# Cross-attention by autocorrelation with a mixture-of-experts layer: skewed copies folded by VectorE, one product a sum instead of two

## The reference, cut to what matters

```python
qf = jnp.fft.rfft(qt)
kf = jnp.fft.rfft(kt)
c = qf.real * kf.real + 1j * -(qf.imag * kf.imag)
corr = jnp.fft.irfft(c, n=Lq)
...
mean_value = jnp.mean(corr, axis=(1, 2))
weights, delay = jax.lax.top_k(mean_value, top_k)
tmp_corr = jax.nn.softmax(weights, axis=-1)
```

## Time and profile before

| what | value |
|---|---|
| three runs | 997.3, 999.38, 1002.05 us; median 999.38 |
| profiled execution, its own time | 996.96 us |
| its span in the trace | 995.1 us |
| granted PE clock, share of full | 0.999 |
| PE busy | 983.5 us (99%) |
| DVE, ACT, POOL busy | 655.4, 380.2, 473.6 us |
| moved by DMA | 216.93 MB, mean 218 GB/s |

### The profile page before, as it was taken

The page is one execution under the profiler, slowest core; times in us unless marked ns, Lnnn a source line. Parts: engine busy times, 40 slices in busy tenths (PEclk is TensorE's granted clock), DMA queues, the critical chain, the costliest instruction groups (busy, mean ns, idle before and its releaser), DMA issues.

```text
span 995.1 us, 21034 instructions
## 1 busy us (share of the span) xinstructions
PE 983.5 (99%) x6750; PEld 601.8 (60%) x6750; DVE 655.4 (66%) x1506; ACT 380.2 (38%) x776; POOL 473.6 (48%) x540
## 2 busy tenths in 40 slices
PE   9999999999999999989999999999999999999998
PEld 7776644444444445557777778777777544444443
DVE  4977788874498898965555555555555476676766
ACT  3646454343545333324444444444444311111111
POOL 0725412131145477654445444444543376666672
PEclk9999999999999999999999999999999999999999
DMA  9735867868562711558889988889988578999675
GB/s 348 259 126 196 295 193 233 233 192 237 175 180 96 222 64 64 127 147 248 251 248 239 256 242 249 242 249 233 261 250 230 169 238 260 313 260 307 187 226 177
DMA packets 175483, 216.93 MB, mean 218 GB/s; under 512 B 101096, under 2 KB 112232, under 8 KB 174376
## 3 DMA queue, kind: packets, MB, share of 16 engines
q1 hardware_dynamic: 151640, 136.95, 46.8%
q0 software_dynamic: 23760, 78.79, 26.8%
HBM read 123.67 MB, written 69.22 MB: 194 GB/s over the span
## 4 chain that ended last, share of the span: by engine, by line
PE 81%; DVE 9%; DMA 4%; issue 3%; ACT 2%; SPq 0%; POOL 0%; DVEq 0%; ACTq 0%; POOLq 0%
PE bank L1068 19%; PE bank L941 13%; PE bank L1131 13%; PE bank L1092 9%; PE bank L957 7%; PE bank L1144 6%; PE bank L1051 5%; PE bank L716 2%; PE bank L1082 2%; PE bank L793 1%; DMA arena<-in_x 1%; DMA arena<-xr_dram 1%; PE bank L696 1%; DVE arena L1855 1%; DVE arena L1622 1%
## 5 line engine op out<-in xcount | busy, mean ns | idle before, releaser
L1068 PE MATMUL bank<-arena 128*128 x1716 | 211.0, 273 | 0.9 <-issue 0.7
L941 PE MATMUL bank<-arena 128*128 128x512 f16 x888 | 202.3, 379 | 0.5 <-DVE arena L1616 0.2
L1068 PEld LDWEIGHTS bank<-arena 128*128 128x128 f16 x1716 | 163.0, 98 | 26.1 <-issue 1.4
L2139 POOL DMA_INDIRECT arena<-y_dram,arena x128 | 135.7, 1060 | 77.9 <-issue 28.9
L2082 POOL DMA_INDIRECT arena<-xr_dram,arena x143 | 139.6, 976 | 59.4 <-issue 48.2
L941 PEld LDWEIGHTS bank<-arena 128*128 128x128 f16 x888 | 87.2, 99 | 100.9 <-DVE arena L1616 0.7
L1131 PE MATMUL bank<-arena 128*128 128x512 f16 x648 | 144.1, 379 | 0.6 <-DMA arena<-xr_dram 0.6
L1092 PE MATMUL bank<-arena 128*128 x429 | 115.4, 378 | 0.5 <-ACT arena L1401 0.5
L1884 DVE SCALAR_TENSOR_TENSOR arena<-bank,arena 128x128 f32<-128x128 f32 x143 | 41.7, 292 | 109.5 <-ACT arena L1390 108.7
L1338 ACT ACTIVATE arena<-arena 128x512 f16<-128x512 f32 x64 | 40.3, 629 | 184.4 <-DVE arena L1616 104.5
L1951 DVE SCALAR_TENSOR_TENSOR arena<-arena 128x512 f32<-128x512 f32 x128 | 95.3, 749 | 23.1 <-DMA arena<-y_dram,arena 20.5
(11 more groups left out here) (227 smaller groups left out, 1318.9 us busy)
## 6 DMA issues: line engine op xcount, KB each, us to landing
y_dram<-arena SPq DMA_DIRECT2D x143, 256.0 KB
arena<-in_x SPq DMA_DIRECT2D x8, 1024.0 KB, 12.0
xr_dram<-arena SPq DMA_DIRECT2D x16, 512.0 KB, 3.9
x_dram<-arena SPq DMA_DIRECT2D x8, 1024.0 KB, 5.6
arena<-in_gu_w SPq DMA_DIRECT2D x16, 512.0 KB, 3.5
out<-arena SPq DMA_DIRECT2D x32, 256.0 KB, 3.8
arena<-x_dram SPq DMA_DIRECT2D x5, 1024.0 KB, 6.0
arena<-in_gu_w POOLq DMA_DIRECT2D x8, 512.0 KB, 4.7
```

What stands on the lines that cost most here:

```text
L941: last = mm(bank[half][:, :], (gu_hi_s, gu_lo_s)[wp][:, c, at:at + H], xt[:, xv * KC + kc, :], start=(n == 0), stop=(n == 3 * KC - 1))
L1068: last = mm(gate_up_bank(s, s)[:, 0:2 * H], rows[:, xv * KC + kc, :], only((gu_hi_r, gu_lo_r)[wp], e, slice(kc * 2 * H, (kc + 1) * 2 * H)) ...
L2139: pool.indirect_dma_start(out=ybuf[n % RING][:, e, :], out_offset=None, in_=y_dram[:, :], in_offset=bass.IndirectOffsetOnAxis(ap=row_of[:, ...
```

## The change

It does the following.

- The two skewed copies are read by halves: partitions 0 to 63 of both tensors (now `skew_near`, `skew_far`) hold the copy shifted one way, its first and its second 64 rows; partitions 64 to 127 hold the other copy in the same manner. For batch 0, where the two lie side by side, one DMA of 64 partitions fills both (`skew_both`); for batch 1 each DMA is split in two: four early reads by GpSimd for two, six late ones by SP for three.
- VectorE adds `skew_far` onto `skew_near` (`fold_part`, a tensor_tensor in f32): for batch 0 in three steps of 768, 512 and 128 + 640 columns, for batch 1 in two, of 1,280 and of 128 + 640.
- `skewed_sum` is one product, with a column of ones and one of ones and minus ones.
- PE's order changes: batch 0's sums are gathered behind the folds, the transposes of block 4 come ahead of the first sums, value parts move behind; the mean correlation comes one value part earlier. In batch 1 the first three sums stand at the end of chunk 0, nine in the first half of chunk 1 and four in its second.
- VectorE's router constants move from ahead of block 5's normalisation to behind `vo_low(0)`.
- GpSimd: blocks 0 to 3 first, then (once the even parts are saved) three tiles of block 4, the first weights, the last tile of block 4 and block 5, then the early reads of batch 1, and only then block 6.

```diff
-SUM_AT = {(0, 0, 10): 1, (0, 0, 11): 2, **{(0, 1, n): i + 3 for i, n in enumerate((0, 1, 3, 4, 6, 7, 9, 10))},
-          (1, 0, 11): 0, **{(1, 1, n): n + 11 for n in range(NA - 11)}}
+SUM_AT = {**{(0, 1, n): n - 8 for n in range(9, 12)}, **{(1, 0, n): n + 4 for n in range(7)},
+          (1, 0, 10): 0, (1, 0, 11): 11, **{(1, 1, n): n + 12 for n in range(NA - 12)}}
+FOLD = P // 2
...
-                sp.dma_start(skew_c[0][:, max(lo - M, 0):hi - M], skewed(0, 2 * M - 1, PTW - 1, max(lo - M, 0), hi - M)
-                             ).then_inc(s_sk[0], 16)
-                sp.dma_start(skew_d[0][:, max(lo, M):hi], skewed(0, 1, PTW + 1, max(lo, M), hi)).then_inc(s_sk[0], 16)
+                sp.dma_start(skew_both[0:FOLD, :, max(lo - M, 0):hi - M],
+                             skewed(0, 2 * M - 1, PTW - 1, max(lo - M, 0), hi - M)).then_inc(s_sk[0], 16)
+                sp.dma_start(skew_both[FOLD:P, :, max(lo, M):hi], skewed(0, 1, PTW + 1, max(lo, M), hi)).then_inc(s_sk[0], 16)
...
-                mm(dst, skew_c[b][:, a * P:a * P + P], c_sb[:, C_ONES + 2 - SUM_W:C_ONES + 2], start=True, stop=False)
-                return mm(dst, skew_d[b][:, a * P:a * P + P], c_sb[:, C_ONES + 4 - SUM_W:C_ONES + 4], start=False, stop=True)
+                return mm(dst, skew_near[b][:, a * P:a * P + P], c_sb[:, C_ONES + 4 - SUM_W:C_ONES + 4],
+                          start=True, stop=True)
...
             second_g(0)
-            pe.wait_ge(s_sk[0], 32)
-            second_g_and_sum(1, (1, 2))
-            skewed_sum(0, 3)
+            second_g(1)
             turn_first(4)
-            for a in (4, 5, 6):
+            pe.wait_ge(s_fold, 1)
+            second_g_and_sum(2, (1, 2, 3, 4))
+            for a in (5, 6):
                 skewed_sum(0, a)
-            pe.wait_ge(s_sk[0], 64)
-            second_g_and_sum(2, (7, 8))
-            second_g_and_sum(3, (9, 10))
+            pe.wait_ge(s_fold, 2)
+            second_g_and_sum(3, (7, 8, 9, 10))
...
-            pe.wait_ge(s_sk2[0], 48)
-            value_part_and_sum(0, (0, 11, 12))
-            summed = value_part_and_sum(1, (13, 14, 15))
+            value_part(0, bank[5], 0)
+            pe.wait_ge(s_fold, 3)
+            for a in (0, *range(11, NA)):
+                summed = skewed_sum(0, a)
             summed.then_inc(s_u, 1)
-            value_part(0, bank[5], 2)
+            value_part(0, bank[5], 1)
             pe.wait_ge(s_tables, 32)
             pe.wait_ge(s_mm_sb, 14)
             even_parts(0)
+            value_part(0, bank[5], 2)
+            mean_correlation(0)
             value_part(0, bank[5], 3)
-            mean_correlation(0)
...
-                    if g == half == 0 and n == 10:
-                        pe.wait_ge(s_sk[1], 32)
+                    if g == 0 and half == 1 and n == 9:
+                        pe.wait_ge(s_fold, 4)
                         pe.wait_ge(s_pt_sb, 7)
-                    if g == 1 and half == 0 and n == 11:
-                        pe.wait_ge(s_sk2[1], 48)
+                    if g == 1 and half == 0 and n == 10:
+                        pe.wait_ge(s_fold, 5)
...
+            def fold_part(b, lo, hi):
+
+                near = skew_near[b][:, lo:hi]
+                return V.tensor_tensor(near, near, skew_far[b][:, lo:hi], ALU.add)
+
+            def fold_late(b):
+
+                dve.wait_ge(s_sk2[b], 96 if b else 48)
+                fold_part(b, 0, M)
+                fold_part(b, EARLY - M, L).then_inc(s_fold, 1)
...
             normalise(4)
-            dve.wait_ge(s_misc, 64)
...
+            for n, (lo, hi) in enumerate(STEPS[0]):
+                dve.wait_ge(s_sk[0], 32 * (n + 1))
+                fold_part(0, max(lo, M) if n == 0 else lo - M, hi - M).then_inc(s_fold, 1)
             V.memset(ones_row[0:1, :], 1.0)
...
             normalise(5)
+            fold_late(0)
             save_sums(0)
...
                     x1_tile(ATTEND[g], 2, 6)
+                if g == 0:
+                    fold_late(1)
                 dve.wait_ge(s_shh, g + 1)
...
             x1_moments(1)
+            dve.wait_ge(s_sk[1], 64)
+            fold_part(1, M, EARLY - M).then_inc(s_fold, 1)
             shared_weights_lo(1)
...
-            for q in range(5):
+            for q in range(HALF):
                 add_bo(q)
+            pool.wait_ge(s_ev_sb, 3)
+            add_bo(4, (0, 1, 2))
             pool.wait_ge(s_mm, 18)
             pool.wait_ge(s_st[0], 16)
             for n in range(2):
                 shared_weights_in(n)
+            add_bo(4, (3,))
             add_bo(5)
-            pool.wait_ge(s_lo0, TB)
-            add_bo(6)
             pool.wait_ge(s_pte, 16)
             pool.wait_ge(s_u, 1)
             pool.wait_ge(s_mm, 28)
-            pool.dma_start(skew_c[1][:, 0:EARLY - M], skewed(1, 2 * M - 1, PTW - 1, 0, EARLY - M)).then_inc(s_sk[1], 16)
-            pool.dma_start(skew_d[1][:, M:EARLY], skewed(1, 1, PTW + 1, M, EARLY)).then_inc(s_sk[1], 16)
+            for v, dst in enumerate((skew_near[1], skew_far[1])):
+                pool.dma_start(dst[0:FOLD, 0:EARLY - M], skewed_half(1, 2 * M - 1, PTW - 1, 0, EARLY - M, v)
+                               ).then_inc(s_sk[1], 16)
+                pool.dma_start(dst[FOLD:P, M:EARLY], skewed_half(1, 1, PTW + 1, M, EARLY, v)).then_inc(s_sk[1], 16)
+            pool.wait_ge(s_lo0, TB)
+            add_bo(6)
             pool.wait_ge(s_wlo, 1)
             shared_weights_in(2)
             add_bo(7)
...
-            pool.wait_ge(s_sk2[1], 48)
+            pool.wait_ge(s_sk2[1], 96)
```

More of the change, by code:

```diff
@@ L106, in constants @@
     c[:, C_ID:C_ID + P] = eye
-    c[:, C_ONES:C_ONES + 4] = [1, 1, 1, -1]
+    c[:, C_ONES:C_ONES + 4] = 1
+    c[FOLD:, C_ONES + 3] = -1
     c[0, C_J0] = 1
@@ L176, in build @@
         xnT = [view(o + 64 * KB, [KC, BLK]), view(o + 72 * KB, [KC, BLK])]
-        skew_c = [view(o + 80 * KB, [L]), view(o + 88 * KB, [L])]
-        skew_d = [view(o + 88 * KB, [L]), view(24 * KB, [L])]
+        skew_near = [view(o + 80 * KB, [L]), view(o + 88 * KB, [L])]
+        skew_far = [view(o + 88 * KB, [L]), view(24 * KB, [L])]
+        skew_both = view(o + 80 * KB, [2, L])
         xtb_c = view(o + 80 * KB, [2, 2 * KC, BLK], F16)
@@ L320, in skewed, with skewed_half @@
         def skewed(b, start, pitch, first, end):
-            return bass.AP(pt_dram, b * P * PTW + start + first, [[pitch, P], [1, end - first]])
+            return bass.AP(pt_dram, b * P * PTW + start + first, [[pitch, FOLD], [FOLD * pitch, 2], [1, end - first]])
+        def skewed_half(b, start, pitch, first, end, v):
+            return bass.AP(pt_dram, b * P * PTW + start + v * FOLD * pitch + first, [[pitch, FOLD], [1, end - first]])
         s_const, s_tables, s_kw2 = sem("identity_in"), sem("tables_in"), sem("wk_in_2")
@@ L472, in skew_late @@
                 sp.wait_ge(s_ptw[b], 16 * (2 if b else len(STEPS[0]) + 2))
-                sp.dma_start(skew_c[b][:, EARLY - M:L], skewed(b, 2 * M - 1, PTW - 1, EARLY - M, L)).then_inc(s_sk2[b], 16)
-                sp.dma_start(skew_d[b][:, EARLY:L], skewed(b, 1, PTW + 1, EARLY, L)).then_inc(s_sk2[b], 16)
-                sp.dma_start(skew_d[b][:, 0:M], skewed(b, 1, PTW + 1, 0, M)).then_inc(s_sk2[b], 16)
+                if b == 0:
+                    sp.dma_start(skew_both[0:FOLD, :, EARLY - M:L], skewed(0, 2 * M - 1, PTW - 1, EARLY - M, L)
+                                 ).then_inc(s_sk2[0], 16)
+                    sp.dma_start(skew_both[FOLD:P, :, EARLY:L], skewed(0, 1, PTW + 1, EARLY, L)).then_inc(s_sk2[0], 16)
+                    sp.dma_start(skew_both[FOLD:P, :, 0:M], skewed(0, 1, PTW + 1, 0, M)).then_inc(s_sk2[0], 16)
+                else:
+                    for v, dst in enumerate((skew_near[1], skew_far[1])):
+                        sp.dma_start(dst[0:FOLD, EARLY - M:L], skewed_half(1, 2 * M - 1, PTW - 1, EARLY - M, L, v)
+                                     ).then_inc(s_sk2[1], 16)
+                        sp.dma_start(dst[FOLD:P, EARLY:L], skewed_half(1, 1, PTW + 1, EARLY, L, v)).then_inc(s_sk2[1], 16)
+                        sp.dma_start(dst[FOLD:P, 0:M], skewed_half(1, 1, PTW + 1, 0, M, v)).then_inc(s_sk2[1], 16)
             def candidates_in(b):
@@ L744, in second_g_and_sum @@
                                 lambda k: column(kT, k, 1), tiles)
-            def value_part_and_sum(c, tiles):
-                return project_and_sum(bank[5][:, c * M:c * M + M], lambda k: wv_sb[:, k, c * P:c * P + P],
-                                       lambda k: column(ctx_sb, k, 0), tiles)
             def second_k(c):
@@ L1561, in _ @@
             vo_low(0)
+            dve.wait_ge(s_misc, 64)
+            dve.wait_ge(s_const, 16)
+            r3 = rt32.rearrange("p (k e) -> p k e", k=KC)
+            link.done(V.tensor_scalar(rt_hi, r3, WS, None, ALU.mult))
+            V.scalar_tensor_tensor(rt_lo, r3, WS, rt_hi, ALU.mult, ALU.subtract).then_inc(s_rt, 1)
+            V.tensor_copy(id16, c_sb[:, C_ID:C_ID + P]).then_inc(s_rt, 1)
```

(10 more changed lines are left out.)

17 lines of the change are left out of this document (3 added, 14 removed).

## The result

The changed kernel took 1013.83 us (median of 6 runs, 1011.41 to 1019.65), the kernel before beside it 999.18 us (6 runs, 997.30 to 1002.65): ratio 1.0143, 95% interval 1.0118 to 1.0167. Forecast were 999.8 us and a range of 995.5 to 1003.0.

A forecast was written before the change was run, and what follows sets the result against it. TensorE, 99% busy, was taken as the bound, but batch 1's chain over GpSimd, ScalarE and VectorE as deciding: +1.6 us there, -1.24 us behind it, +0.4 on 999.38 gives 999.8 us, range 995.5 to 1003.

The forecast's parts named there:

- Folds, batch 0: VectorE's folds in batch 0: 2.5 us of work, each paying up to one 1 us wait; PE loses 0.2 and 2.2 us.
- Fold 2: Batch 0's second fold on VectorE: ends near 47.1, PE wants it at 47.6, so no wait.
- the late reads: Batch 0's last skewed reads on SP's queue: issued up to 47.16, landing 3.0 us later, at 50.2.
- the late fold: Batch 0's last fold, after block 5's normalisation on VectorE: ends at 52.5, PE ready at 50.3, 2.2 us lost.
- fold 1: Batch 0's first fold, 768 columns on VectorE: ends near 45.3, PE arrives at 45.15, 0.2 us of waiting.
- GpSimd's and VectorE's queue, batch 1: Batch 1's chain from GpSimd's reads, adds and weights 2 through VectorE to block 2's attention product: PE gets there 1.6 us later.
- in time: Batch 1's early reads, last issued at 96.5, land 5.1 us later at 101.6, before VectorE's fold could start at 102.8.
- 1.9 + 1.6 = 3.5: First attention product 1.9 us earlier, that of block 2's second tile 1.6 us later than before: the forecast loss between them.
- Rival 2: Reads of 64 partitions at half rate, batch 1's early ones taking 10.2 us, not 5.1: +2.8 us, 1002.2; chance 0.15.
- Rival 3: PE's order and VectorE's folds in batch 0 lose over 2.2 us, first attention product gains nothing: +2.3 us, 1001.7; chance 0.10.
- the constants moved into VectorE's gap: Router's split and other constants, 9 instructions, in VectorE's idle 4.54 us ahead of 78.39: cost nothing, without that gap 1.5 us.
- rival 1: Neither batch's chain holds PE, so the full saving of 5.9 to 7.1 us comes: 992.3 to 993.5; chance 0.10.

The follow-up runs named there:

- the filled kernel: The changed kernel with idle products on TensorE sized to its waits, two and three in batch 0, 22 short ones in batch 1: 1008.12 us, ratio 1.0081.
- a clean pause of 3.1: The kernel before, with TensorE alone made to wait for VectorE's router constants ahead of a second-batch product, no transfer changed: 1013.79 us, ratio 1.0136.
- the two-queue kernel: The changed kernel with batch 0's transfers to partitions 64 to 127 issued by ScalarE's queue instead of SP's: 1017.50 us, ratio 1.0144.
- The same wait, unfilled and filled: The kernel before with a wait for VectorE's router constants added, alone (1013.79 us) or with three idle products ahead of it (1003.17 us).
- the one with 1.1: The kernel before with the added wait for VectorE's router constants put one second-batch product later, a shorter pause: 1008.15 us, ratio 1.0047.
- the pause kernels: The kernel before with an added TensorE wait: unfilled 1013.79 us, with three idle products ahead 1003.17 us, one product later 1008.15 us.
- the kernel with batch 1 later: The change for batch 1 alone, against the kernel before, fold behind the first low weights and all sums in chunk 1: 1001.92 us, ratio 1.0033.

## Why the prediction was wrong

**Folds, batch 0: "Fold 2 ends near 47.1, PE wants it at 47.6: covered."** This is the step that failed first. I costed the fold and GpSimd's collisions and let the reads land as before. The write ahead of them took 5.0 in place of 2.7 us, its reads were issued at 43.5 in place of 40.9, and fold 2 ended at 49.7. The same goes for "the late reads are issued up to 47.16 and land 3.0 us later, at 50.2": SP issued the last at 50.48, and VectorE began the late fold at 54.57, forecast to end at 52.5. I had expected 2.2 us of waiting there and 0.2 at fold 1; 1.70 at fold 2 and 0.40 there came instead, so the sum of the waiting, 2.1 us, was nearly right and its place wrong.

**The term that the sum lacked: the clock.** The forecast held that a wait costs its length. It can cost more: 5 us of batch 0's 7.4 by the filled kernel, 11 us for a clean pause of 3.1. A pause of 1.70 us set it off in the changed kernel, whose six runs all have a mean clock of 0.985 to 0.990, so the 2.2 us in one piece that I forecast would probably have done so with every landing on time; no run shows that case. The longest pause in the rows of before is 0.70 us, with no fall of the clock behind it: nothing there priced it, but a forecast of 2.2 us of idle time on an engine that had none was the place to ask.

**GpSimd's and VectorE's queue, batch 1.** The chain of queues ran as told, with sizes off, but it held TensorE at another place: the forecast had it wait for the SiLU and L1569, and the rows show 5.17 and 1.07 us for the folds and 0.51 for the attention add (L1594 here). Taking off the 7.4 us of batch 0, weights 2 were issued 6.1 us later than before (forecast 4.0): the write of batch 1's correlation went out at 91.8, not 90.6, and took 5.0 us, not 4.2. The early reads needed 7.8 us, not 5.1, and landed at 113.9, which is 106.5 without the shift, not 101.6: "in time" was wrong by 4.9 us. The fold took 3.77 us, not 1.5, beside the adds. TensorE then idled 6.8 us between 112 and 128 (I had said 4 to 7), and from the first attention product to that of block 2's second tile it lost 6.8 us, where 1.9 + 1.6 = 3.5 was forecast. The half clock behind the pause makes 1.3 of that, by the starts of the same work at full clock; with the 6.8 us of waiting, 0.8 lost ahead of chunk 0 and 2.3 saved by the products removed up to there, that is 6.6.

**Rival 2, reads at half rate,** was given 0.15 and placed in batch 1 alone. The rate was the right worry: 202 to 254 GB/s against 382 to 412. In batch 0 the second write, its reads and the late ones stand behind one another on SP's queue, so each slow read delays all that follows; there I did not look. In batch 1 its own sign came true: it was to decide once the reads need over 6.3 us, and they needed 7.8. Its argument against, that transfers to both halves are in flight together, fell with the two-queue kernel.

**Rival 3, batch 0 loses,** was given 0.10. It named the right place, but priced it at 1.9 us, for folds that meet GpSimd's adds; the first attention product came 8.5 us later than forecast (84.05 against 75.6), by late reads and the clock.

**What held:** 3.6 us of products in batch 0 (the filled kernel's sum closes with it to 0.3 us), and in batch 1 0.22 us a sum (a sum with its product takes 0.36 us behind 121.77, and took 0.58 behind 114.85); the constants moved into VectorE's gap cost nothing (it idles 3.76 us behind them); the full saving (rival 1) did not come, for the reason given.

## What to carry to other kernels

On an engine that is 99% busy, ask of every new wait first whether it makes a pause: in this kernel pauses of 1.5 to 3.5 us brought from some 7 to 24 us at half clock, and the two cases that were priced cost 5 and 11 us beyond the waiting. Don't make such a pause, or fill it. Idle products kept the clock, but their own time ate much of what they saved; filling with work that is due anyway was not tried here. Carry a slower transfer through the whole chain that shares its queue, and when a tile is packed by halves of the partitions, lay the two parts out by even and odd ones.

## What the runs showed of the hardware

The same wait, unfilled and filled, differed by 10.6 us of 1000. How long the half clock lasts does not follow the pause: 1.54 and 1.70 us were followed by some 14 and 17 us of it, 3.08 by 24, 3.94 and 5.17 us in batch 1 by 7 and 3.5. Kernels whose profiles show pauses of 0.85 and 1.1 us and a full clock are a lottery: ten runs of the one with 1.1 gave 1001.2 to 1010.4 us, in step with a mean clock of 1.0 to 0.990. The kernel before shows the same thing, mildly, with no wait added: of 27 runs beside the pause kernels, 15 had a mean clock of 1.0 (998.0 to 1003.7 us), and the three at 0.995 to 0.997 took 1008.9 to 1009.7.

Interleaving even and odd partitions raised the rate of the changed kernel's reads from about 230 to about 360 GB/s with the same number of transfers and bytes. VectorE's add of 1,280 columns took 2.90 to 4.84 us in eight profiles where GpSimd's adds ran beside it, and 1.48 us in the kernel with batch 1 later, where they did not.
